# Windowed-attention layers on one core: copies ahead of exponentials, TensorE's steps reordered, scores in 64 by 96 tiles, the x split moved

## The reference

```python
for i in range(DEPTH):                                  # 6
    x = attn_layer(shift_tokens(x), Wqkv[i], q_scale[i], k_scale[i], Wo[i]) + x
    x = ffn_layer(shift_tokens(x), ln_g[i], ln_b[i], W1[i], b1[i], W2[i], b2[i]) + x
```

## Time and profile before

| | |
|---|---|
| median of 3 runs | 4904.15 us (4900.57 to 4906.80) |
| the profiled execution | 4893.89 us, its span 4892.1 us |
| busy: PE, DVE, ACT, POOL | 3937.6, 3707.1, 3320.4, 2839.3 us (80, 76, 68, 58%) |
| weight loads (PEld) | 2525.8 us |
| mean granted TensorE clock | 0.874 |
| DMA | 351.70 MB, one hardware queue busy 20.4% |

### The profile page before, as it was taken

How to read it: one execution, slowest core, us unless ns; L and a number is a source line. 1 busy time by engine, 2 the same in 40 slices (tenths; PEclk the granted TensorE clock), 3 DMA queues, 4 the chain that set the end, 5 groups by cost and what they waited for, 6 DMA issues and landing times.

```text
span 4892.1 us, 97213 instructions
## 1 busy us (share of the span) xinstructions
PE 3937.6 (80%) x24672; PEld 2525.8 (52%) x24672; DVE 3707.1 (76%) x12335; ACT 3320.4 (68%) x8937; POOL 2839.3 (58%) x4494
## 2 busy tenths in 40 slices
PE   4555548988888888788888888888888887888885
PEld 2223225655555555555555555555555555555553
DVE  7778768877777777677777777777777776777873
ACT  2222227878777777677777677786777776777774
POOL 2222237766566666566666566665666665666661
PEclk6555559999989999899999999999999998999997
DMA  1000012222222222222222222222222222222221
GB/s 40 4 4 2 4 58 92 85 79 85 83 85 76 81 82 85 79 83 81 80 80 85 83 85 75 82 82 86 86 75 85 75 90 79 86 79 78 86 71 58
DMA packets 225175, 351.70 MB, mean 72 GB/s; under 512 B 41534, under 2 KB 68348, under 8 KB 224380
## 3 DMA queue, kind: packets, MB, share of 16 engines
q1 hardware_dynamic: 224604, 345.22, 20.4%
HBM read 125.41 MB, written 5.77 MB: 27 GB/s over the span
## 4 chain that ended last, share of the span: by engine, by line
PE 39%; ACT 24%; DVE 12%; issue 10%; DMA 1%; ACTq 1%; POOL 0%; DVEq 0%; SPq 0%; POOLq 0%
ACT pr L745 11%; PE bank L279 6%; PE bank L583 5%; PE bank L594 5%; DVE sm L1106 4%; PE bank L281 4%; PE bank L280 4%; PE bank L551 3%; DVE ab L1060 3%; PE bank L564 2%; ACT L766 2%; PE bank L555 2%; ACT wide L754 2%; PE bank L565 1%; PE bank L537 1%
## 5 line engine op out<-in xcount | busy, mean ns | idle before, releaser
L745 ACT ACTIVATE pr<-sm,nb,rq 128x128 f32<-128x128 f32 (+1 forms) x3072 | 1520.4, 496 | 726.5 <-DVE nb L1112 704.7
L862 POOL TENSOR_SCALAR pr<-pr,rden 128x128 f32<-128x128 f32 (+1 forms) x3072 | 1133.4, 389 | 1259.8 <-DVE rden L1085 1258.9
L1060 DVE TENSOR_TENSOR ab<-bank,ltab 128x512 f32<-128x512 f32 x1536 | 985.4, 683 | 235.2 <-PE bank L281 208.0
L1106 DVE CUSTOM_DVE_ANT_0 sm<-bank,mask 128x128 f32<-128x128 f32 (+1 forms) x3072 | 844.8, 331 | 348.4 <-issue 296.5
L869 POOL TENSOR_TENSOR rot<-ab,swp 128x512 f32<-128x512 f32 x768 | 981.1, 1277 | 65.9 <-DMA swp<-ab 59.5
L733 ACT ACTIVATE sq<-bank 128x512 f32<-128x512 f32 x768 | 450.2, 586 | 262.6 <-DVE ab L1060 259.7
L564 PE MATMUL bank<-ident,pr 128*128 128x128 f32 x1536 | 439.1, 311 | 196.2 <-DVE pt L1092 195.7
L745 ACT ACTIVATION_READ_ACCUMULATOR pr<-sm,nb,rq 128x1 f32 x3072 | 575.6, 187 | 0.0
L551 PEld LDWEIGHTS bank<-rot 64*128 64x128 f32 x3072 | 241.1, 192 | 640.5 <-issue 436.2
L1092 DVE COPY pt<-bank 128x512 f32<-128x512 f32 x768 | 531.5, 692 | 10.3
L551 PE MATMUL bank<-rot 64*128 64x128 f32 x3072 | 392.0, 333 | 172.5 <-DVE nb L1112 151.1
(11 more groups left out here) (153 smaller groups left out, 7420.5 us busy)
## 6 DMA issues: line engine op xcount, KB each, us to landing
swp<-ab SPq DMA_DIRECT2D x1536, 128.0 KB, 2.0
rkb<-k_scratch SPq DMA_DIRECT2D x768, 128.0 KB, 2.9
raw<-Wqkv SPq DMA_DIRECT2D x48, 128.0 KB, 2.2
gg<-xT SPq DMA_DIRECT2D x48, 128.0 KB, 2.7
gg<-xT SPq DMA_DIRECT2D x48, 127.5 KB, 2.6
raw<-Wqkv SPq DMA_DIRECT2D x12, 256.0 KB, 2.8
wo<-Wo SPq DMA_DIRECT2D x6, 512.0 KB, 4.0
k_scratch<-rsum SPq DMA_DIRECT2D x192, 8.0 KB
```

The lines of the kernel that those rows point to most:

```text
L745: ins = act.activation(pr[:, s % 4, i, cs], sm[:, s % 2, i, cs], ACT.Exp, bias=nb[:, s, t, i:i + 1], scale=head_scale(rq, p, b)[:, t, i:i ...
L862: ins = pool.tensor_scalar(pr[:, e % 4, i, cs], pr[:, e % 4, i, cs], rden[:, e, t, i:i + 1], 1.0, ALU.mult, ALU.mult)
L1060: ins = dve.tensor_tensor(seqs(ab[:, j % 2, i, :]), seqs(use_bank("qk", j)[:, :]), ltab[:, 2 * (j % 2) + i:2 * (j % 2) + i + 1, :] .to_bro ...
L1106: ins = dve.tensor_tensor_reduce(sm[:, s % 2, i, cs], bank[i][:, cs], mask[:, cs], 1.0, -3e38, ALU.add, ALU.max, mx[:, t, i:i + 1])
```

## The change

Five things. (1) On TensorE each step now runs: scores; the f32 work (down, bank of `wo`, norm transposes, centring; the other two downs; `project_out`); transposes; outputs or V; then QK, gate, up and variance; square sums. The banks in `BANK_STEPS` are dealt out anew. (2) Scores are computed in four tiles of 64 queries by 96 keys for each head, in place of two with 128 queries by 128 and 160 keys; the two banks are zeroed once at the start, since parts of them are no longer written. (3) ScalarE copies outputs or V before the exponentials of the step. (4) The split of x moves from the steps 8 and 9 to 11, 13 and 14. (5) Some key scalings and their spreads come one step earlier. In `scores` the waits' values are computed ahead.

```diff
-BANK_STEPS = [[("next", "qk", 0, 4), ("prev2", "dn", 0, 5)],
-              [("next", "qk", 1, 6)],
-              [("next", "qk", 2, 4), ("prev", "wo", 0, 6)],
-              [("next", "qk", 3, 4)],
-              [("next", "qk", 4, 5), ("cur", "rqT", 1, 4)],
+BANK_STEPS = [[("prev2", "dn", 0, 4), ("next", "qk", 0, 5)],
+              [("next", "qk", 1, 5)],
+              [("prev", "wo", 0, 6), ("next", "qk", 2, 5)],
+              [("next", "qk", 3, 5)],
+              [("cur", "rqT", 1, 4), ("next", "qk", 4, 5)],
               [("next", "qk", 5, 5)],
               [("next", "qk", 6, 4)],
-              [("next", "qk", 7, 5), ("prev", "cen", 0, 6)],
-              [("next", "qk", 8, 4), ("prev", "var", 0, 5)],
-              [("next", "qk", 9, 4)],
-              [("next", "qk", 10, 5)],
-              [("next", "qk", 11, 4), ("next", "rqT", 0, 6)],
-              [("next", "qk", 12, 5), ("prev", "g", 0, 4)],
+              [("prev", "cen", 0, 6), ("next", "qk", 7, 5)],
+              [("next", "qk", 8, 5), ("prev", "var", 0, 4)],
+              [("next", "qk", 9, 5)],
+              [("next", "qk", 10, 4)],
+              [("next", "rqT", 0, 6), ("next", "qk", 11, 5)],
+              [("prev", "g", 0, 4), ("next", "qk", 12, 5)],
               [("prev", "g", 1, 6), ("prev", "g", 2, 4), ("next", "qk", 13, 5)],
               [("prev", "a", 0, 6), ("prev", "a", 1, 4), ("next", "qk", 14, 5)],
               [("next", "qk", 15, 5), ("prev", "a", 2, 6)]]
...
-SPREAD_STEPS = {0: ("cur", 3), 4: ("cur", 4), 5: ("cur", 5), 8: ("cur", 6), 10: ("cur", 7),
+SPREAD_STEPS = {0: ("cur", 3), 4: ("cur", 4), 5: ("cur", 5), 7: ("cur", 6), 9: ("cur", 7),
...
-SCALE_STEPS = {13: [("cur", 7), ("next", 0)], 15: [("next", 1)], 1: [("cur", 2)], 3: [("cur", 3)], 7: [("cur", 4)],
-               9: [("cur", 5)], 11: [("cur", 6)]}
+SCALE_STEPS = {13: [("next", 0)], 15: [("next", 1)], 1: [("cur", 2)], 3: [("cur", 3)], 6: [("cur", 4)],
+               8: [("cur", 5)], 10: [("cur", 6)], 12: [("cur", 7)]}
+SCORE_TILES = [(0, 0, 0), (1, 32, 32), (2, P, P - WINDOW), (3, P + 64, P + 32)]
...
-                    for i in range(2):
-                        rows = slice(64 * i, 64 * i + 64)
-                        pe.matmul(bank[i][:, 0:P], rot[rows, p, c0:c0 + P], rot[rows, PAIRS + p, c0:c0 + P],
-                                  start=True, stop=True)
-                    for i in range(2):
-                        rows = slice(64 * i, 64 * i + 64)
-                        mm = pe.matmul(bank[i][:, P:UW], rot[rows, p, c0 + P:c0 + SEQ],
-                                       rot[rows, PAIRS + p, c0 + P - WINDOW:c0 + SEQ], start=True, stop=True)
+                    for half, c, k0 in SCORE_TILES:
+                        part = slice(64 * (half % 2), 64 * (half % 2) + 64)
+                        for i in range(2):
+                            rows = slice(64 * i, 64 * i + 64)
+                            mm = pe.matmul(bank[i][part, c:c + 96], rot[rows, p, c0 + 64 * half:c0 + 64 * half + 64],
+                                           rot[rows, PAIRS + p, c0 + k0:c0 + k0 + 96], start=True, stop=True)
...
                     if cur is not None:
                         scores(s)
+                    bank_work(s, ("dn", "wo", "rqT", "cen"))
+                    if s in (1, 2) and prev2 is not None:
+                        down(s, prev2)
+                    if WO_STEP <= s < WO_STEP + NWO and prev is not None:
+                        project_out(s - WO_STEP, prev)
                     if s < 3 and prev is not None:
                         transpose_probs(s + 13, prev)
...
                         make_v(s)
-                    for role, what, i, _ in BANK_STEPS[s]:
...
-                    if s in (1, 2) and prev2 is not None:
-                        down(s, prev2)
-                    if WO_STEP <= s < WO_STEP + NWO and prev is not None:
-                        project_out(s - WO_STEP, prev)
+                    bank_work(s, ("qk", "g", "a", "var"))
                     if s in QUAD_STEPS and group_of(QUAD_STEPS[s][0], o) is not None:
...
                 for s in range(16):
-                    if cur is not None:
-                        probabilities(s)
                     if s % 2 == 0 and s < 6 and prev is not None:
                         copy_outputs(s // 2 + 5, prev)
                     if s % 2 == 0 and s >= 6 and cur is not None:
                         copy_outputs(s // 2 - 3, cur)
                     if s in V_STEPS and group_of(V_STEPS[s][0], o) is not None:
                         copy_v(V_STEPS[s][1], group_of(V_STEPS[s][0], o))
+                    if cur is not None:
+                        probabilities(s)
...
-                    if gs[2] is not None and s == 8:
+                    if gs[2] is not None and s == 11:
                         if cur is not None:
                             dve.wait_ge(v_proj, n8 + 8)
                         split_high_x(gs[2], par)
-                    if gs[2] is not None and s == 9:
-                        split_low_x(gs[2], par, n1 + 3 if cur is not None else n1 + 2)
+                    if gs[2] is not None and s in (13, 14):
+                        split_low_x(gs[2], par, n1 + 3 if cur is not None else n1 + 2, s - 13)
...
+            for i in range(2):
+                dve.memset(bank[i][:, :], 0.0)
```

More of the change, by code:

```diff
@@ L544, in scores @@
                     p, b = s // 2, s % 2
+                    scaled = held(pe, n8 + (p + 1))
+                    used = held(pe, n16 + s)
+                    settle(pe)
                     if b == 0:
[L546 to L547 removed]
+                        pe.wait_ge(k_norm, scaled)
+                    pe.wait_ge(sc_bias, used)
                     c0 = b * SEQ
[L549 to L556 removed]
+                    for half, c, k0 in SCORE_TILES:
[4 more added lines that the diff above has]
+                                           rot[rows, PAIRS + p, c0 + k0:c0 + k0 + 96], start=True, stop=True)
                     mm.then_inc(sc_ps, 1)
@@ L624, in down, with bank_work @@
                         mm.then_inc(f_dn, 1)
-                k = 0
+                def bank_work(s, whats):
+                    k = sum(len(step) for step in BANK_STEPS[:s])
+                    for b, (role, what, i, _) in enumerate(BANK_STEPS[s]):
+                        q = group_of(role, o)
+                        if what not in whats or q is None:
+                            continue
+                        free_bank(k + b)
+                        bk = use_bank(what, i)
+                        if what == "qk":
+                            project(i, q, bk)
+                        elif what == "rqT":
+                            q_norms(i, q, bk)
+                        elif what == "cen":
+                            centre(q, bk)
+                        elif what == "var":
+                            variance(q, bk)
+                        elif what in ("g", "a"):
+                            up(("a", "g").index(what), i, q, bk)
+                        elif what == "dn":
+                            down(0, q)
                 for s in range(16):
@@ L1038, in split_high_x, with split_low_x @@
                 dve.tensor_copy(xh[64:128, buf, :, 1:SEQ], src[64:128, :, 0:SEQ - 1]).then_inc(x_hi, 1)
-            def split_low_x(g, buf, count):
+            def split_low_x(g, buf, count, half):
                 src = seqs(xT[:, bass.ds(g * GT, GT)])
-                dve.wait_ge(x_hi, count)
-                dve.tensor_tensor(xl[0:64, buf, :, :], src[0:64], xh[0:64, buf, :, :].bitcast(F32), ALU.subtract)
-                dve.tensor_tensor(xl[64:128, buf, :, 1:SEQ], src[64:128, :, 0:SEQ - 1],
-                                  xh[64:128, buf, :, 1:SEQ].bitcast(F32), ALU.subtract).then_inc(x_split, 1)
+                if half == 0:
+                    dve.wait_ge(x_hi, count)
+                    dve.tensor_tensor(xl[0:64, buf, :, :], src[0:64], xh[0:64, buf, :, :].bitcast(F32), ALU.subtract)
+                else:
+                    dve.tensor_tensor(xl[64:128, buf, :, 1:SEQ], src[64:128, :, 0:SEQ - 1],
+                                      xh[64:128, buf, :, 1:SEQ].bitcast(F32), ALU.subtract).then_inc(x_split, 1)
             def turn(n, o, par, gs, kind, l):
@@ L1188, in _ @@
             split_high_x(0, 0)
-            split_low_x(0, 0, CREDIT + 1)
+            for half in range(2):
+                split_low_x(0, 0, CREDIT + 1, half)
             layer_tables(0)
```

19 lines of the change are left out of this document (removed).

## The result

| | before | after |
|---|---|---|
| median | 4902.67 us (4 runs, 4900.57 to 4906.80) | 5085.11 us (4 runs, 5078.37 to 5092.74) |
| ratio after/before | | 1.0372, 95% interval 1.0354 to 1.0389 |
| profiled execution, its span | 4893.89, 4892.1 us | 5078.37, 5076.5 us |
| mean granted TensorE clock | 0.874 | 0.862 |

A forecast was written before the change was run, and what follows sets the result against it. No engine is full; TensorE is busiest, below full clock, and waits add. Terms -3.5 + 1.3 + 0.4 + 2.7 + 0.8 - 0.5 + 1.4 = +2.6 us a turn, +125 over 48 turns, -10 for weight loads: 5019 us, range 4850 to 5120.

The forecast's parts named there:

- the clock in steps 3 to 8: TensorE's clock falls to half behind new waits in steps 3 and 7: +1.4 us a turn, bounds 0 and +3.4.
- the split in step 12: Pieces of the x split moved to DVE's steps 11, 13 and 14 stay covered: 0; without cover, 2.2 us a turn.
- steps 9 to 11: Chain from scores(9) to scores(11) keeps its length less the faster scores; less work at half clock in step 11: -0.5 us.
- steps 13 to 15: Later exponentials and step savings turned into waits give back +0.4 us of the tile gain.
- Scores block: Scores on four 64x64 tiles, four abreast: 0.48 us instead of 0.69, -0.21 us a step, -3.5 us a turn.
- rival with two abreast: Scores tiles run two abreast or at 71 ns a pair: +5 to +10 us a turn, 5230 to 5450 us; chance 0.08.
- ScalarE's order, step 2: Late outputs copy holds exponentials, norms and the square QK(3) needs; QK(3) starts at t(2) + 11.85: +1.3 us.
- Centring: Centring, now first in step 7, waits 3.1 us for the shifted x: +2.7 us a turn, the largest term.
- Rival B: Faster: shifted x has landed when TensorE reaches centring in step 7; 4830 us, or 4795 with full clock; chance 0.22.
- V's wait: Step 7: V's 0.5 us wait for the output copy goes, subtracted from centring's 3.1 us wait.
- QK(8)'s wait: Late V(7) delays its copy, exponentials and squares, so QK(8), using the same bank, waits: +0.8 us.
- Turns that load weights: Five such turns have transpose waits in steps 1 and 2, partly filled by f32 work: some 2 us each, -10.

The follow-up runs named there:

- third experiment: ScalarE's exponentials put ahead of the copies again, in the kernel after: 5017.47 us, ratio 1.0232.
- the ninth: TensorE's new step order and new banks alone, on the kernel before: 4996.01 us, ratio 1.0194.
- second experiment: Centring put back last in step 7, behind QK(7), in the kernel after: 4917.82 us, ratio 1.0036.
- fifth: Key spread of pair 5 issued in SP's step 6 in place of 5, behind the two shifts, in the kernel after: 5012.64 us, ratio 1.0226.
- sixth experiment: Two matmuls of constants with unused results put ahead of centring in step 7, in the kernel after: 5027.95 us, ratio 1.0256.
- fourth: Split of x put back in DVE's steps 8 and 9, in the kernel after: 5007.54 us, ratio 1.0210.
- eleventh experiment: Split of x moved to steps 11, 13 and 14 and nothing else, on the kernel before: 4950.65 us, ratio 1.0098.
- the best kernel: Scores tiles and ScalarE's copies ahead of the exponentials, nothing else, on the kernel before: 4718.94 us, ratio 0.9622.

## Why the split costs

Timelines of DVE and GpSimd at one split: the kernel with the split alone (the two casts of step 11 and GpSimd beside them), the kernel before (step 8; DVE, then GpSimd), and after (DVE, then GpSimd):

```profile
2597.86 1.28 POOL L875 TENSOR_TENSOR rot<-rot,rkb 128x512 f32<-128x512 f32 x1
...
2598.54 0.89 DVE L1037 CAST xh<-xT 64x512 fp32r x1
...
2599.11 1.47 POOL L891 TENSOR_TENSOR xn_l<-gg,xn_h 128x512 fp32r<-128x512 f32 x1
...
2599.44 1.42 DVE L1038 CAST xh<-xT 64x510 fp32r x1
```
```profile
2549.54 0.42 DVE L1037 CAST xh<-xT 64x512 fp32r x1
2549.97 0.42 DVE L1038 CAST xh<-xT 64x510 fp32r x1
```
```profile
2550.78 1.48 POOL L862 TENSOR_SCALAR pr<-pr,rden 128x128 f32<-128x128 f32 x4 [1.76 <-DVE rden L1085]
```
```profile
2651.02 1.45 DVE L1044 CAST xh<-xT 64x512 fp32r x1
2652.48 0.42 DVE L1045 CAST xh<-xT 64x510 fp32r x1
```
```profile
2650.92 1.27 POOL L898 TENSOR_TENSOR xn_l<-gg,xn_h 128x512 fp32r<-128x512 f32 x1 [0.52 <-ACT xn_h L831]
```

The cast takes 0.42 us alone and 1.42 or 1.45 when GpSimd has begun an operation just before it; it ends some 0.3 us after GpSimd's (2599.11 + 1.47 = 2600.58 and 2599.44 + 1.42 = 2600.86; 2652.19 and 2652.47). None of these DVE rows shows a wait for a semaphore. Over all casts of four traces (before, after, the split alone, the split back) this holds without exception: the 145 casts that start while a GpSimd operation runs end 0.275 to 0.289 us after that operation, however much of it was left, and the 239 others take 0.41 to 0.43 us. Among those are the 21 in after during which GpSimd starts only later. For the subtractions it is 106, ending 0.54 to 0.55 us after GpSimd's operation, and 278 others at 0.67 to 0.69. What it costs in after, TensorE in step 12:

```profile
2654.24 0.30 PE L566 MATMUL bank<-ident,pr 128*128 128x128 f32 x1 [0.55 <-DVE pt L1101]
```

In this turn the wait is 0.55 us. The copy of transposed probabilities stands behind the casts in DVE's queue, and the transposes wait for it. Over the execution (duration in ns min/median/max of one line, first and last start): the second cast before and with the split alone, the first cast of after and of after with the split back, the subtraction before and after:

```profile
L1038 DVE CAST xh<-xT x48: 423/424/426, 672.0 to 4616.1; 64x510 fp32r<-64x510 f32 x24, 64x510 fp32r x24
```
```profile
L1038 DVE CAST xh<-xT x48: 423/1413/1423, 672.0 to 4695.9; 64x510 fp32r<-64x510 f32 x24, 64x510 fp32r x24
```
```profile
L1044 DVE CAST xh<-xT x48: 407/932/1462, 671.3 to 4814.6; 64x512 fp32r<-64x512 f32 x24, 64x512 fp32r x24
```
```profile
L1044 DVE CAST xh<-xT x48: 407/419/1049, 671.6 to 4738.7; 64x512 fp32r<-64x512 f32 x24, 64x512 fp32r x24
```
```profile
L1043 DVE TENSOR_TENSOR xl<-xT,xh x48: 673/673/1065, 672.4 to 4621.4; 64x512 fp32r<-64x512 f32 x48
```
```profile
L1051 DVE TENSOR_TENSOR xl<-xT,xh x48: 673/1242/1830, 672.2 to 4823.8; 64x512 fp32r<-64x512 f32 x48
```

Where the split stood, GpSimd isn't idle (it is busy for 67% and 86% of the steps 8 and 9 before), but at the moment of the split it is: the casts at 2549.54 lie in the 1.76 us in which GpSimd waits for DVE's reciprocal, which stands behind them in DVE's queue. Where the split went, GpSimd's operation has already begun. The Trainium skill ("SBUF — State Buffer", section "Who interferes with whom") says that VectorE and GpSimd share one pair of SBUF ports, held for a whole instruction, and that casts in VectorE's two-port mode and operations with two SBUF inputs block on it. These rows agree: the cast's end follows GpSimd's at one distance. No run here moved only the GpSimd operation, so the port itself is the page's explanation, and what is shown is that the two ends go together.

## Why the prediction was right, and where it was off

The sign, the place and most sizes were right; the sum was too small by 2.0 us an ordinary turn (forecast +2.6, measured +4.63). The errors have both signs: the clock in steps 3 to 8 (+1.5), the split in step 12 (+1.1) and half clock in step 0 (+0.3) against centring with QK(8) (-0.6) and steps 9 to 11 (-0.3). So part of the nearness is luck. By steps (the forecasts sum to 2.8 here, not 2.6: the prediction took -3.5 for the tiles, and 16 times its -0.21 is -3.4, and the rest is rounding):

```
part of the turn        forecast, us   measured, us   of it clock (half of the added half-clock time)
steps 0 to 3              +0.4           +0.86          0.3 (step 0) + 0.37 (step 3)
steps 4 to 6              -0.6           +0.41          1.05
steps 7 and 8             +3.1           +4.02          1.5
steps 9 to 11             -1.1           -1.41          -0.8, in the forecast's -0.5
step 12                   -0.2           +0.94
steps 13 to 15            -0.2           -0.18
clock, steps 3 to 8       +1.4           (above)        2.9
```

- **Scores block.** 0.48 forecast, 0.49 measured; four abreast. The rival with two abreast (0.66 us for the streams alone), or at the outputs' 71 ns a pair, falls: sixteen pairs in 0.49 us are 31 ns each. The Trainium skill ("TensorE: Matmul & The Clock Gate", section "Back-to-back issue gap") gives about 81 ns for one of a stream of weight-load and matmul pairs of 128 columns; this block's pairs, of 96 columns on four tiles, don't go at that pace.
- **ScalarE's order, step 2.** QK(3) was to start at t(2) + 11.85 and wait 2.6 us; it starts at + 11.93 and waits 2.58. (The prediction's first paragraph calls the wait before 1.6 us; the row says 1.35, and 1.35 + 1.3 gives the 2.6.) The third experiment removes it, the ninth shows that it needs both the grouping and the order.
- **Centring.** Rival B's condition (the shift has landed) is not met: QK(5) at t(5) + 3.45 (forecast 3.4), swap at + 5.67 (5.6), wait in every turn. The wait is 3.09 us in the mean of the ordinary turns, where 3.1 was forecast. In the turn shown centring starts at + 12.87 where 11.9 was forecast, because the transfer took 3.8 us, the maximum of the earlier trace rows; in the next turn the wait is only 2.47 us. V's wait, forecast to give back 0.5, was 0.26 in the mean. Without the clock, steps 7 and 8 cost 4.02 - 1.5 = 2.5 us, less than the 3.1 of the sum: QK(8)'s wait, forecast at 0.8, is 0.4 in the mean. Moving centring (second experiment) and moving one spread (fifth) confirm the mechanism.
- **Clock: the mis-sized term.** I took 1.4, between bounds of 0 and 3.4. It is (0.73 + 2.10 + 3.06) / 2 = 2.9 (3.06 are the added half-clock us of steps 7 and 8): behind the wait of QK(3) half clock follows in 19 of 29 turns, behind centring's in 22. Against 1.4 that is 1.5 of the 2.0 us. The bounds held and the choice of the middle was too low. That each wait is followed by either clock from turn to turn, at one length of 2.58 us, the rows of the kernel before don't show; what decides it stays open. The sixth experiment prices it in step 7 alone.
- **The x split: priced at 0, costs 1.1.** "In steps 11, 13 and 14 its pieces (0.85, 0.67, 0.69 us) lie on DVE steps of 3.7 us": the durations came from a place where GpSimd was idle. Beside GpSimd, in after, the two casts take up to 1.9 us together and a subtraction up to 1.8 (1.2 in the median), and "hidden" looked only at DVE's sum per step and not at who stands behind the casts in its queue, which is the copy that step 12's transposes wait for. The fourth and the eleventh experiment show it from both sides (-78 and +52 us).
- **Steps 9 to 11** gained slightly more than forecast; the chain from scores(9) to scores(11) took 11.59 us (forecast 11.48). Steps 13 to 15 came out as forecast.
- **Turns that load weights.** Five were to gain 2 us each in steps 1 and 2, where the f32 work fills waits at the transposes. The five T2 turns do gain there, and more: step 2 falls from 9.70 to 5.73 us and step 1 from 6.14 to 5.53. In the five T0 turns the two steps together fall from 14.65 to 11.96. Step 7 takes it back, 4.07 to 8.55 in T2 and 4.65 to 8.56 in T0, and T0 pays 1.9 more in step 8 and 2.5 in step 12. On balance they are 1.5 and 2.8 us longer, less than an ordinary turn's 4.63.

Whether the moved scalings cost or gain by themselves was not run alone; the fifth experiment shows that the spread in step 5, which the change left in its place, costs beside centring, and the best kernel leaves them all where they were.

## What to carry over

When work is regrouped on the busiest engine, list for every block that moved forward what feeds it and when that lands, and for every block that moved back who is waiting behind it: here one block of 1 us, moved ahead of its transfer, was 167 of some 326 us of losses, and filling a part of its wait with matmuls of nothing made the kernel 57 us faster. An operation's duration belongs to its place: before moving DVE work with both ends in SBUF, look at what GpSimd does at that very moment in the new step: a step in which it is busy for 86% still had a free place. Take a change apart before rejecting it: of these five parts two are worth 3.8% together, and the other three on top of them cost more than that (4718.94 to 5085.11 us).

## What the runs showed of the hardware

- A DVE cast or subtraction between SBUF tiles that starts while a GpSimd operation runs ends 0.28 or 0.54 us after that operation, in all 251 cases; casts so take up to 1.46 us in place of 0.42, subtractions up to 1.83 in place of 0.67. A GpSimd operation that starts during a cast left it at 0.42 (21 cases).
- Sixteen f32 matmul instructions on 64x64 tiles of 96 columns take 0.49 us at full clock. At the transposes' rate the streams alone would be 0.66 us two abreast and 0.33 four abreast (an estimate), so more than two go side by side, and the eight extra weight loads didn't make the block longer than the 0.69 us it took before.
- The clock: in step 15 of before, with V's wait of 1.61 us, it stayed at 1.00 in all 29 turns; in the kernel with the tiles alone, with 1.83 us in the same place, it was at 0.50 for up to 3.4 us in 27. A wait of 2.58 us was followed by 0.50 in 19 of 29. Extra matmuls inside centring's idle time left half clock behind it in 4 turns of 29 in place of 22. So a saving in front of a wait is not always neutral: 3.4 us at half clock are 1.7 us of work.
